# Reciprocal square roots by one power operation on GpSimd, in a transformer block followed by linear attention

## The reference

```
rmsnorm(x, w): v = mean(x*x, last axis);  w * x * rsqrt(v + 1e-6)
h   = rmsnorm(x, n1) * (1 + scale) + shift
q,k,v = h @ qkv_w.T, in 16 heads of 8 features
q,k = rmsnorm over each head's 8 features, then a rotation by position
x   = x + gate * (softmax(q k^T / sqrt(8)) v) @ proj_w.T
h2  = rmsnorm(x, n2) * (1 + scale) + shift
x   = x + gate * ((silu(h2 @ w1.T) * (h2 @ w3.T)) @ w2.T)
```

## Time and profile before

| | before |
|---|---|
| median of three runs | 277.94 us (277.62 to 278.91) |
| span of the profiled execution, first to last instruction | 274.4 us |
| around the span, to the median of the runs | 3.5 us |
| VectorE busy | 220.0 us, 80% of the span, 700 instructions |
| TensorE busy | 214.6 us, 78% |
| ScalarE busy | 169.7 us, 62% |
| GpSimd busy | 158.6 us, 58%, 431 instructions |
| mean granted TensorE clock | 0.900 |

### The profile page before, as it was taken

The page is one execution under the profiler, slowest core; times in us unless marked ns, Lnnn a source line. Parts: engine busy times, 40 slices in busy tenths (PEclk is TensorE's granted clock), DMA queues, the critical chain, the costliest instruction groups (busy, mean ns, idle before and its releaser), DMA issues. The chain is left out here.

```text
span 274.4 us, 7061 instructions
## 1 busy us (share of the span) xinstructions
PE 214.6 (78%) x2028; PEld 162.0 (59%) x2028; DVE 220.0 (80%) x700; ACT 169.7 (62%) x437; POOL 158.6 (58%) x431
## 2 busy tenths in 40 slices
PE   3406196998999989889899999599994899756763
PEld 2403053777677767767677777488882588533531
DVE  7495979899999999999999962587888899946322
ACT  0526235789898989889898875324340377654661
POOL 6184778888888887778887500011207486785300
PEclk9999565699999999999999999979999799995555
DMA  7710000000000000000000000000000000000112
GB/s 147 207 36 0 2 0 0 4 2 0 4 4 4 0 0 0 0 0 0 0 4 0 2 2 1 1 4 0 0 0 0 0 4 1 2 0 0 39 38 76
DMA packets 9554, 4.01 MB, mean 15 GB/s; under 512 B 2669, under 2 KB 9530, under 8 KB 9530
## 3 DMA queue, kind: packets, MB, share of 16 engines
q1 hardware_dynamic: 4170, 2.18, 2.9%
q10 hardware_dynamic: 5360, 1.54, 2.4%
HBM read 2.67 MB, written 1.05 MB: 14 GB/s over the span
## 5 line engine op out<-in xcount | busy, mean ns | idle before, releaser
L1268 DVE TENSOR_REDUCE nmax<-bank 128x4 f32<-128x512 f32 x64 | 42.6, 682 | 2.5 <-PE bank L1468 2.0
L1062 ACT ACTIVATE probs<-bank 128x512 f32<-128x512 f32 x64 | 37.6, 603 | 4.4 <-PE bank L1454 4.3
L1453 PE MATMUL bank<-qT,kT 128*128 128x128 bf16 x256 | 34.6, 222 | 0.3
L1454 PE MATMUL bank<-mT,sel 128*128 128x128 bf16 x256 | 34.5, 222 | 0.0
L1453 PEld LDWEIGHTS bank<-qT,kT 128*128 128x128 bf16 x256 | 25.4, 100 | 4.0 <-ACT mT L1095 1.3
L1454 PEld LDWEIGHTS bank<-mT,sel 128*128 128x128 bf16 x256 | 25.5, 99 | 2.8 <-issue 2.5
L1468 PE MATMUL bank<-kT,qT 128*128 128x256 bf16 x128 | 25.4, 282 | 0.6 <-DVE nmax L1268 0.6
L430 POOL TENSOR_TENSOR xs<-x,rstd 128x256 f32<-128x256 f32 x8 | 4.8, 612 | 32.6 <-DVE rstd L396 19.0
L543 ACT ACTIVATE th<-bank 128x256 f32<-128x256 f32 x24 | 9.2, 384 | 21.0 <-PE bank L776 11.1
L1498 PE MATMUL bank<-identb,parts 128*128 128x128 bf16 x256 | 20.8, 228 | 1.5 <-DVE kT L1350 0.9
L1498 PEld LDWEIGHTS bank<-identb,parts 128*128 128x128 bf16 x256 | 17.5, 104 | 5.2 <-DVE parts L1291 2.5
(11 more groups left out here) (247 smaller groups left out, 683.0 us busy)
## 6 DMA issues: line engine op xcount, KB each, us to landing
out_dram<-res SPq DMA_DIRECT2D x4, 256.0 KB, 2.3
xin<-in_x_dram ACTq DMA_DIRECT2D x1, 768.0 KB, 8.3
ada_n<-in_L_cond_ada_w_dram ACTq DMA_DIRECT2D x1, 384.0 KB, 3.7
xin<-in_x_dram ACTq DMA_DIRECT2D x1, 256.0 KB, 4.1
w_n<-in_L_cond_w_dram SPq DMA_DIRECT2D x2, 128.0 KB
qkv_n<-in_L_cond_qkv_w_dram SPq DMA_DIRECT2D x1, 192.0 KB, 4.5
w_n<-in_L_cond_w_dram SPq DMA_DIRECT2D x1, 170.5 KB
emb_n<-in_L_cond_emb_W_dram SPq DMA_DIRECT2D x1, 128.0 KB
```

The costliest lines, as they stand in the source:

```text
L1062: q.activation(probs[c][:, :, :].rearrange("p h t -> p (h t)"), bank[E_BANK[c % 2]][:, :], ACT.Exp, scale=SCALE).then_inc(s_p, 1)
L1268: q.tensor_reduce(nmax[q1][:, c * HPC:(c + 1) * HPC], bank[S_BANK[c % 2]][:, :].rearrange("p (h t) -> p h t", t=T), X_AXIS, ALU.max, negat ...
L1453: q.matmul(dst, kT[q0][:, h // 2, h % 2, :], qT[q0][:, h // 2, :], start=True, stop=False)
L1454: last = q.matmul(dst, sel[:, h, :], mT[q0][:, :], start=False, stop=True)
```

## The change

Every root becomes one GpSimd instruction, `tensor_tensor` with the operation `pow` and a tile `minus_half` that holds -0.5. The guess and the Newton steps are taken out on both engines. The mean squares are no longer halved. Where VectorE made the root of a second half, GpSimd now makes it, ahead of unit 4; the input's roots move from VectorE to GpSimd as well, the first (sequences 0 to 3) ahead of the two `affine_select` of `sel`, the second (4 to 15) at step -1, where GpSimd takes over the input norm. Two waits are new on GpSimd (`b_xsT`, `c_xsT`, ahead of stages C and D).

```diff
-        def rsqrt(v, sm, base, y_, s_, t_):
-            ...
-            did(nc.vector.tensor_scalar(t_.bitcast(I32), s_.bitcast(I32), 1, None, ALU.logical_shift_right))
-            did(nc.vector.tensor_scalar(y_.bitcast(I32), t_.bitcast(I32), -1.0, float(MAGIC), ALU.mult, ALU.add))
-            for _ in range(3):
-                did(nc.vector.tensor_tensor(t_, y_, y_, ALU.mult))
-                did(nc.vector.scalar_tensor_tensor(t_, t_, -0.5, s_, ALU.mult, ALU.mult))
-                did(nc.vector.scalar_tensor_tensor(y_, t_, 1.5, y_, ALU.add, ALU.mult))
...
+            def root(sm, rstd, cols, n):
+
                 g.wait_ge(sm, n)
+                q.tensor_tensor(rstd[:, cols], ms[:, cols], minus_half[:, cols], ALU.pow).then_inc(sm, 1)
...
             g.wait_ge(s_bn, EARLY)
-            half_square(b_rstd, None, EPS0)
-            for k in range(3):
-                newton(b_rstd, rstd1, k)
-            g.wait_ge(b_rstd, 18)
+            mean_square(b_rstd, None, EPS0)
+            root(b_rstd, rstd1, early, 4)
+            g.wait_ge(b_rstd, 5)
...
                 if at(t, EARLY_U):
+                    root(b_late, rstd1, late, RSTEPS - 1)
                     g.wait_ge(b_late, RSTEPS)
...
+            root(c_rstd, rstd2, early, 4)
+            g.wait_ge(c_rstd, 5)
+            g.wait_ge(b_xsT, U)
...
                 if at(t + 3, EARLY_U):
+                    root(c_late, rstd2, late, LSTEPS - 1)
                     g.wait_ge(c_late, LSTEPS)
...
                 if at(t, EARLY_U):
                     g.wait_ge(c_bn, EARLY_U)
-                    half_square(d_rstd, mean3, EPS1)
-                for k in range(3):
-                    if at(t, EARLY_U + 1 + k):
-                        newton(d_rstd, rstd3, k)
+                    mean_square(d_rstd, mean3, EPS1)
+                    root(d_rstd, rstd3, early, 4)
...
                 if at(t, EARLY_U):
+                    root(d_late, rstd3, late, LSTEPS - 1)
                     g.wait_ge(d_late, LSTEPS)
...
+            def input_root(rows, ready):
+
+                g.wait_ge(pv_v, ready)
+                q.tensor_tensor(rstd_x[:, rows], ms[:, rows], minus_half[:, rows], ALU.pow).then_inc(s_rx, 1)
+
+            input_root(slice(0, HEAD_B), V_MS)
...
                 g.wait_ge(s_ss, SEED * b + SEED)
-                for k in range(3):
-                    q.tensor_tensor(t_, y_, y_, ALU.mult).then_inc(s_newton, 1)
-                    ...
-                    q.tensor_tensor(y_, y_, t_, ALU.mult).then_inc(s_newton, 1)
-                    g.wait_ge(s_newton, NEWT * b + 4 * k + 4)
+                q.tensor_tensor(qv_y[p][:, :], qv_s[p][:, :], minus_half[:, :], ALU.pow).then_inc(s_root, 1)
+                g.wait_ge(s_root, ROOT * b + ROOT)
...
                     if k == 1:
-                        q.tensor_scalar(qv_s[q0][:, :], qv_ms[q0][:, :], 0.5 / DH, 0.5 * EPS0, ALU.mult, ALU.add).then_inc(s_ss, 1)
-                    if k == 2:
-                        q.tensor_scalar(qv_ms[q0][:, :].bitcast(I32), qv_s[q0][:, :].bitcast(I32), 1, None,
-                                        ALU.logical_shift_right).then_inc(s_ss, 1)
-                    if k == 3:
-                        wait(v, s_rot, ROT * (b - 2) + ROT)
-                        q.tensor_scalar(qv_y[q0][:, :].bitcast(I32), qv_ms[q0][:, :].bitcast(I32), -1.0,
-                                        float(MAGIC - 2 ** 22), ALU.mult, ALU.add).then_inc(s_ss, 1)
+                        v.wait_ge(s_ss, SEED * b + 1)
+                        wait(v, s_root, ROOT * (b - 2) + ROOT)
+                        q.tensor_scalar(qv_s[q0][:, :], qv_ms[q0][:, :], 1.0 / DH, EPS0, ALU.mult, ALU.add).then_inc(s_ss, 1)
```

More of the change, by code:

```diff
@@ L276, in dit_then_linear_attention @@
         pv_g = sem("pv_g")
+        s_rx = sem("s_rx")
         s_xs = sem("s_xs")
@@ L415, in blocks_gpsimd @@
             q = nc.gpsimd
+            early, late = slice(0, EARLY), slice(EARLY, B)
             def normed(src, mean, rstd, centred, made, used):
@@ L459, in half_square @@
                 g.wait_ge(sm, 1)
-                q.tensor_scalar(m_, m_, 0.5 / D, 0.5 * eps, ALU.mult, ALU.add)
+                q.tensor_scalar(m_, m_, 1.0 / D, eps, ALU.mult, ALU.add)
                 if mean is None:
@@ L466, in half_square @@
                 g.wait_ge(sm, 2)
-                q.tensor_scalar(r_, r_, 0.25 if mean is None else 0.125, 0.0, ALU.mult, ALU.add).then_inc(sm, 1)
+                q.tensor_scalar(r_, r_, 0.5 if mean is None else 0.25, 0.0, ALU.mult, ALU.add).then_inc(sm, 1)
                 g.wait_ge(sm, 3)
@@ L511, in c_step @@
                     g.wait_ge(c_bn, EARLY_U)
-                    half_square(d_rstd, mean3, EPS1)
-                for k in range(3):
-                    if at(t, EARLY_U + 1 + k):
-                        newton(d_rstd, rstd3, k)
+                    mean_square(d_rstd, mean3, EPS1)
+                    root(d_rstd, rstd3, early, 4)
             units(g, c_step, 3)
-            g.wait_ge(d_rstd, 18)
+            g.wait_ge(d_rstd, 5)
+            g.wait_ge(c_xsT, U)
             d_normed = normed(y, mean3, rstd3, d_xc, d_xs, d_xsT)
@@ L636, in late_rms, with late_std @@
                 q.scalar_tensor_tensor(m_, r_, 0.5, m_, ALU.mult, ALU.add).then_inc(b_late, 1)
-                v.wait_ge(b_late, 3)
-                assert rsqrt(v, b_late, 3, rstd1[:, late], m_, r_) == RSTEPS
-            def late_std(mean, rstd, sm):
+            def late_std(mean, sm):
                 q.tensor_tensor(mean[:, late], me, mo, ALU.add)
@@ L974, in step @@
                 if at(t, POOL_NORMS):
-                    g.wait_ge(pv_v, V_RSTDS)
+                    input_root(slice(HEAD_B, B), V_MSS)
+                    g.wait_ge(s_rx, 2)
                 input_normed(t, p)
@@ L995, in step @@
                 g.wait_ge(s_ss, SEED * b + SEED)
-                y_, s_, t_ = qv_y[p][:, :], qv_s[p][:, :], qv_t[:, :]
-                for k in range(3):
-                    q.tensor_tensor(t_, y_, y_, ALU.mult).then_inc(s_newton, 1)
-                    g.wait_ge(s_newton, NEWT * b + 4 * k + 1)
-                    q.tensor_tensor(t_, t_, s_, ALU.mult).then_inc(s_newton, 1)
-                    g.wait_ge(s_newton, NEWT * b + 4 * k + 2)
-                    q.tensor_tensor(t_, three_halves[:, :], t_, ALU.subtract).then_inc(s_newton, 1)
-                    g.wait_ge(s_newton, NEWT * b + 4 * k + 3)
-                    q.tensor_tensor(y_, y_, t_, ALU.mult).then_inc(s_newton, 1)
-                    g.wait_ge(s_newton, NEWT * b + 4 * k + 4)
+                q.tensor_tensor(qv_y[p][:, :], qv_s[p][:, :], minus_half[:, :], ALU.pow).then_inc(s_root, 1)
+                g.wait_ge(s_root, ROOT * b + ROOT)
                 g.wait_ge(s_rot, ROT * b + 2)
@@ L1207, in _, with input_ms @@
             assert n == V_MOD
-            def input_rstd(rows):
+            def input_ms(rows):
                 nonlocal n
@@ L1213, in input_rstd, with other_ms @@
                 did(q.tensor_scalar(ms[:, rows], ms[:, rows], 1.0 / D, EPS0, ALU.mult, ALU.add))
-                n = rsqrt(v, pv_v, n, rstd_x[:, rows], ms[:, rows], rt[:, rows])
             v.wait_ge(pv_a, A_SQUARE)
-            input_rstd(slice(0, HEAD_B))
-            assert n == V_RSTD
-            def other_rstd():
+            input_ms(slice(0, HEAD_B))
+            assert n == V_MS
+            def other_ms():
                 v.wait_ge(pv_a, A_SQUARES)
-                input_rstd(slice(HEAD_B, B))
-                assert n == V_RSTDS
+                input_ms(slice(HEAD_B, B))
+                assert n == V_MSS
             def other_modulations():
@@ L1335, in step @@
                     wait(v, s_xsT, b - 1)
+                    if at(t, -LEAD):
+                        v.wait_ge(s_rx, 1)
                     q.tensor_scalar(xs[q1][:, :], xin[:, bass.ds(b, 1), :].rearrange("p a f -> p (a f)"),
@@ L1368, in step @@
                                     xin[:, bass.ds(b, 1), :].rearrange("p a f -> p (a f)"), ALU.add).then_inc(s_x1, 1)
-                seed(2)
                 if is_seq(t - 1):
                     v.wait_ge(s_x1, t)
-                seed(3)
                 if is_seq(t - 1):
@@ L1375, in step @@
                                x1[:, bass.ds(t - 1, 1), :].rearrange("p a f -> p (a f)")).then_inc(s_bn, 1)
-                if at(t, B - LEAD + 1):
-                    early_seed(v, b_rstd, rstd1)
             def step_with_preparation(t, p):
                 step(t, p)
-                for k, prepare in ((-4, other_rstd), (-4, other_modulations),
+                for k, prepare in ((-4, other_ms), (-4, other_modulations),
                                    (-4, style), (-2, biases)):
```

57 lines of the change are left out of this document (10 added, 47 removed).

## The result

The changed kernel takes 287.24 us (285.61 to 289.08, 4 runs), the kernel before beside it 277.78 (276.58 to 278.91): the ratio is 1.035, with an interval of 1.031 to 1.040. The forecast was 263 us. The time lies inside the range of 251 to 291, but the sign is wrong: the change makes the kernel 9.5 us slower. Medians are over all runs of a kernel, ratios over its fast runs alone, those within 1.5% of its fastest.

The account below looks back on a forecast made before the run. VectorE, without gaps in the attention stage, was taken as the bound, GpSimd nearly as full. Terms -8.0 + 0.5 - 0.5 - 3.0 - 1.1 - 2.2 - 0.3 = -14.6 us from 277.94 gave 263 us, range 251 to 291.

Parts of the forecast that it names:

- P: GpSimd's time for one power on 32 columns, estimated at 1.5 us, with 0.5 us for 8 columns.
- Step 4: Steady attention steps: VectorE's savings are waited away behind the power; 7.8 against 7.74 us, +0.5 us over twelve steps.
- 6.27 + P: Attention step length in us when VectorE's L1282 stalls behind the power, not under about 7.2.
- B: Rival: the power is long and VectorE waits behind it every step at L1282, slower from P = 2.7 us; chance 0.28.
- Steps 1 to 3: Start-up: the input's roots and the q and k seeds of sequences 0 to 2 leave VectorE; 8.0 us saved.
- Step 1: Input, sequences 0 to 3: one GpSimd power replaces eleven VectorE instructions; L1336 starts near 16.1, 4.0 us earlier.
- Steps 5 to 7: MLP statistics save 0.5 us, MLP to linear attention 3.0, linear attention to the end 1.1, 2.2 and 0.3.
- A: Rival: the power is cheap, P at most 1.0; step 7.2 to 7.3, about 256.5 us; chance 0.22.
- C: Rival: the power gets the port ahead of VectorE's L1363; step about 6.8 + P, 270 us; chance 0.06 with D.
- D: Rival: the first power also waits for its code, once in the start-up; 267 or near 269 us; chance 0.06 with C.

Follow-up runs that it names:

- e3: Changed kernel with each q and k power replaced by an ordinary 128x3200 GpSimd product plus a 32-column product, roots left out: 353.3 us.
- e1: Changed kernel with the 16 powers of q and k turned into plain products of the same shape, roots left out: 260.83 us, ratio to before 0.939.
- e2: Changed kernel with each q and k power on 16 of 32 columns and a product on the others, whose roots are left out: 259.74 us.
- e5: Changed kernel with each q and k power on 24 columns and a product on the other 8, whose roots are left out: 270.0 us.
- e11: Kernel before with the input's two roots alone by the power: 274.41 us, ratio 0.987.
- e7: Kernel before with the roots of stages B, C and D alone by the power: 273.3 us, ratio 0.981.
- e6: Kernel before with the roots of q and k alone by the power: 291.42 us, ratio 1.047.
- e10: Changed kernel with the q and k roots made as before (VectorE seed, GpSimd Newton steps), all others by the power: 270.43 us, ratio 0.971.

## Why the prediction was wrong

**The price of the power** is the term that gave the wrong sign. "I take 1.5 (call it P) and 0.5" was measured as 5.44 and 1.64. The upper bound was the length of the chain that it replaces, 4.4 us, "though nothing excludes more"; more was the case. The slope of ordinary instructions is 2.2 ns a column, that of the power 158: the "some 20 such passes", for which no row stood, would have had to be some 72.

**Step 4, the steady steps.** Forecast +0.5 us over twelve steps (7.8 each for 7.74). Found: +15.2 by the prediction's own row (9.01 each; the first of the twelve holds the input's second power), and +12.2 from power to power (8.76 each). Two things in it failed. The formula 6.27 + P made VectorE wait behind the power; at P = 5.44 it gives a step of 11.7 and a total of about 310, and the chip shows 8.76 and 287. The rule of the shared port holds for GpSimd's ordinary instructions (e3: 3.83 us for a VectorE instruction that takes 0.62 in the changed kernel; formula 12.2, measured 13.3 for a full step) and not for the power (L1242: 0.28 us inside it). The section "Who interferes with whom" of the page "SBUF — State Buffer" in the Trainium skill has the lock held for a whole instruction; e3 agrees with that, the power's rows don't. What the rows don't settle is why: a power that seldom takes the port would look like this, but no run tests it.

And the step lacked the line that decided: GpSimd's own sum. Its work beside the root is 3.3 us (8.76 - 5.44), so its turn is 3.3 + P, over the floor of 7.3 (e1) from P = 4.0 on and over the 7.59 of the kernel before from about 4.3. The prediction had GpSimd with 2.9 us of room and an idle gap before its rotation; it has neither. The rival that was slower (B) had this side of the sign and the wrong place: L1282 of VectorE, from P = 2.7. At 2.9 (e2, part of the root left out) the kernel is 18 us faster than before, not slower. So the numbers of B near the truth (290 at P = 3.5) are an accident of two errors.

**Steps 1 to 3, the start-up**, forecast -8.0, found -1.8 up to L1258 of sequence 3 and +2.3 at the first statistics. Step 1's instants were nearly right: the power at 15.52, the first L1284 at 16.66 for 16.1, in the changed kernel

```profile
15.52 1.03 POOL L916 TENSOR_TENSOR rstd_x<-ms,minus_half 128x4 f32<-128x4 f32 x1
16.52 4.17 POOL L932 TENSOR_SCALAR_AFFINE_SELECT sel<-sel 128x2048 bf16<-128x2048 bf16 x2
```

but the gain was partly eaten by what moved: L932 (the L970 of before) now lies over VectorE's scaling of the input, where it had lain over a Newton instruction:

```profile
16.66 2.15 DVE L1284 TENSOR_SCALAR xs<-xin,rstd_x 128x128 f32<-128x128 f32 x2 [2.50 <-POOL rstd_x L916]
```

2.15 us for two that took 0.48 together, so the first rotation came at 22.32 instead of 24.10: 1.8 us of the 4.0. The prediction even named where L970 would end, and did not ask whom it would stop. With the long powers gone the start-up gives -6.8 (e1), near the forecast; with them it is GpSimd's again (e5). The input's roots alone are worth 3.7 us in all (e11).

**Steps 5 to 7, behind the attention stage**, forecast -7.1. The traces show -7.8 for the changed kernel, but its profiled run was its fastest; e7, timed, gives -5.4 (-4.2 to -6.6 by its interval). Behind the last statistics the eleven profiled executions with the small powers have 88.0 to 92.9 us, 90.9 in the mean, and the three without (before, e6, e11) 94.8 to 95.8, mean 95.2: -4.3. So the mechanism is right and the sum some 2 us too large. The price of a small power is enough to explain that, though no run separates it: 1.64 for 0.5 us, twice on the chain, in stage C at 231.80 and in stage D at 262.76, which the prediction held for hidden:

```profile
231.80 1.60 POOL rstd L416
...
261.33 1.39 issue
262.76 1.65 POOL rstd L416
```

**Rivals.** A (cheap power, 256.5) is what e1 and e2 come near: 260.8 and 259.7. C fell with the port. D fell: the first power takes 1.03 us at 15.52, on the line through the later ones, so the trace shows no wait for code.

## What to carry to other kernels

Before an operation moves to an engine, add up that engine's own turn, with the gaps between dependent instructions and not its busy share, and find the price at which the turn crosses the floor of the others; when the price is unknown, that crossing is the forecast's real content. One instruction in place of twelve is not shorter for being one: here the power loses on 32 columns (5.4 us against 4.1 to 4.4) and wins on 4 to 12 (1.0 to 2.3 us), where the old root was a chain of small instructions and hand-overs (2.2 us for eleven on 8 columns, 2.5 on 12); so in this kernel it is worth having for the small ones alone (e10, 2.9% faster than before). And a gain in a start-up is only kept if the engine that is full there gets shorter too.

## What the runs showed of the hardware

GpSimd's power (tensor_tensor with the exponent in a tile, f32, 128 partitions) takes 0.39 us and 0.158 us a column: 1.03, 1.64, 2.27, 2.92, 4.18 and 5.44 us for 4, 8, 12, 16, 24 and 32 columns. An ordinary product needs 3200 columns for that time (5.54 us). While it runs, VectorE's instructions with two SBUF operands keep their length (0.17 and 0.28 us); beside a product of the same length the one that met it was stopped to its end (3.83 us in the mean of sixteen). Newton steps on GpSimd cost 0.25 us each and some 0.08 between two of them, which no busy share shows.
